# The experts' up products in one pass over both parts of the rows, with h_low on GpSimd

## The chip, the cores and the metric

One core of one Trainium2 chip. The metric is the device time of one execution in microseconds (us). The kernel before took 968.19 us (median of 3 runs, 966.38 to 971.39). The engines are called PE (TensorE matmul), DVE (VectorE), ACT (ScalarE), POOL (GpSimd) and SP (SyncE, which here issues the weight loads).

## What is computed

A gated cross attention, and then a gated mixture of experts over all 16 x 100 tokens of 512 features. The change touches only the experts:

```python
xs = x * gate                                # gate: sigmoid of the top router logit, top_k = 1
def body(acc, (wg, wd, e)):                  # 8 experts
    g, u = split(xs @ wg)                    # 512 -> 2 x 1024
    o = (silu(g) * u) @ wd                   # 1024 -> 512
    return acc + where(ids == e, o, 0)
routed = scan(body, 0, (w_gate_up, w_down))
shared = (silu(x @ sg) * (x @ su)) @ sd
x = x + tanh(g_ffn) * (routed + shared)
```

All inputs and outputs are fp32. The kernel multiplies in fp32r: it splits each operand into a high part (rounded by a copy to fp32r) and a low part (the difference), and adds the products high x high, high x low and low x high in PSUM.

## The kernel before, in words

The stage that matters is the last one, the routed experts (some 692 to 959 us of the profiled span). Each of the 8 experts is given the tokens routed to it, 2 tiles of 112 rows, 224 columns (SLOTS) once turned. The hidden size 1024 is worked off in four quarters of 256 (FQ), so there are 32 steps n = 4e + q. A step has two halves j = 0, 1 of 128 hidden features.

**PE** (`pe_routed`). In step n, for each half j: the gate product and the up product into PSUM banks 2j and 2j + 1, and after both halves the down product of step n - 1. The gate product (`pe_expert_gate`, L1648) already takes the rows' high and low part side by side: per 128 of the 512 input features one matmul of the weight's high part with 448 columns (rows high and low, L1660) and one of the weight's low part with the 224 columns of the rows' high part (L1662). The left half of the bank then lacks the right half, which must be added. The up product (`pe_gate_up`, L1613) takes three matmuls of 224 columns per 128 features (L1642), 12 in all, all added in PSUM. The down product (L1729) has two tiles of 6 matmuls. Ahead of q = 3 PE turns the next expert's rows (L1948).

**ACT** (`act_routed`), in this order in a step: copy_gate 0 (L1670: the right half of the bank into `hidden[0]`), part_high a, silu 0 (L1683), copy_gate 1, h_high 0 (L1703), part_high b, silu 1, h_high 1, part_high c. part_high (L1590) rounds one 128 x 1024 part of the next step's weights: a is gate, b is up, c is down. At q = 3 two rows_high (L1960) come first.

**DVE** (`dve_routed`): sum_gate 0 (L1677: left half of the bank plus the copy), part_low a (L1597), mult 0 (L1714: up from PSUM times the silu), h_low 0 (L1719), sum_gate 1, part_low b, mult 1, h_low 1, part_low c. At q = 3 two rows_low (L1967) come first; at q = 0 two add_residual (L2099) of the expert before come last.

**POOL** (`pool_routed`): for each expert the gather of the next expert's rows (L1991), the scatter of the last one's output (L2008) and the gather of this one's residual (L2001), all indirect DMAs.

**SP** loads a weight part of 512 KB when the part four before it in order has been split (`sp_load_part`, L1534).

Every engine works its list off in order, and semaphores tie them. Those that matter here: a product waits for part_low of its weights (`w_low`, L1621, L1654) and for the reader of its bank in the step before; h_high waits for mult; part_low for part_high; the down product for both h_low (L1726); copy_gate of half j waits for h_low of the same half in the step before, since `hidden[j]` is overwritten (L1669).

```python
    for i in range(k.KD):
        PE.matmul(bank[:, 0:2 * SLOTS].rearrange("p (x n) -> p x n", x=2), high[:, i, :], xs[:, :, i, 0:SLOTS],
                  start=(i == 0), stop=False)
        made = PE.matmul(bank[:, 0:SLOTS], low[:, i, :], xs[:, 0, i, 0:SLOTS], start=False, stop=(i == k.KD - 1))
```

Of the kernel before, what the change touches and what calls it, by code (L numbers as in the profile page):

```python
# [22 lines left out]
F32 = mybir.dt.float32  # L23
# [6 lines left out]
ACT = mybir.ActivationFunctionType  # L30
AX = mybir.AxisListType
MULT, ADD, SUB = ALU.mult, ALU.add, ALU.subtract

P = 128
# [135 lines left out]
def lay_out(k, nc, stack):  # L170
# [75 lines left out]
    k.w_raw = [carve(P, [PART], F32) for _ in range(2)]  # L246
    k.rows += [carve(P, [D], F32) for _ in range(2)]
    k.hidden = [carve(P, [max(k.width)], F32) for _ in range(2)]
    k.up_first = carve(P, [k.width[0]], F32)
    k.w_raw += [carve(P, [PART], F32), late("w_raw3", [P, PART], F32)]  # L250
    k.w_split = [[[carve_r(P, [PART], F32R) for _ in range(2)] for _ in range(3)]]
    k.xn_both = [xnT0, xnT1]
# [90 lines left out]
def sweep_semaphores(sem, name, it0, u0):  # L343
    r = Sweep()
    r.name, r.it0, r.u0 = name, it0, u0
    r.w_in = [sem(f"{name}_w_in{i}") for i in range(4)]
    r.w_high, r.w_low = sem(f"{name}_w_high"), sem(f"{name}_w_low")
    r.gu, r.silu, r.mult = sem(f"{name}_gu"), sem(f"{name}_silu"), sem(f"{name}_mult")
    r.h_high, r.h_low, r.routed_down = (sem(f"{name}_{n}") for n in ("h_high", "h_low", "routed_down"))
    r.gate_copied, r.gate_summed = sem(f"{name}_gate_copied"), sem(f"{name}_gate_summed")  # L350
    r.ids_in = sem(f"{name}_ids_in")
    r.rows_in = [sem(f"{name}_rows_in{i}") for i in range(4)]
    r.xt_turned, r.xt_high, r.xt_low = (sem(f"{name}_{n}") for n in ("xt_turned", "xt_high", "xt_low"))
    r.residual_in = [sem(f"{name}_residual_in{i}") for i in range(NT)]
    r.y_added = sem(f"{name}_y_added")
    r.y_out = [sem(f"{name}_y_out{i}") for i in range(NT)]
    return r
# [1245 lines left out]
def product_bank(r, it, j, which):  # L1603


    if it >= r.it0:
        return 2 * j + which
    if it < 2:
        return (((3, 2), (0, 2)), ((3, 5), (6, 7)))[it][j][which]
    return which  # L1610
# [34 lines left out]
        made.then_inc(r.gu, 1)  # L1645


def pe_expert_gate(k, r, PE, w, n, j):  # L1648


    it, u, xs = r.it0 + n, r.u0 + n, k.xn_both[n // k.NQ % 2]
    bank = k.bank[product_bank(r, it, j, 0)]
    high, low = (t[:].rearrange("p (k f) -> p k f", k=k.KD)[:, :, P * j:P * j + P] for t in k.w_split[u % 3][0])
    w.wait_ge(r.w_low, 3 * u + 1)  # L1654
    if n:
        w.wait_ge(r.gate_summed, 2 * n + j - 1)
    else:
        w.wait_ge(r.silu, 2 * it)
    for i in range(k.KD):
        PE.matmul(bank[:, 0:2 * SLOTS].rearrange("p (x n) -> p x n", x=2), high[:, i, :], xs[:, :, i, 0:SLOTS],  # L1660
                  start=(i == 0), stop=False)
        made = PE.matmul(bank[:, 0:SLOTS], low[:, i, :], xs[:, 0, i, 0:SLOTS], start=False, stop=(i == k.KD - 1))  # L1662
    made.then_inc(r.gu, 1)


def act_copy_gate(k, r, A, w, n, j):
    it = r.it0 + n
    w.wait_ge(r.gu, 4 * it + 2 * j + 1)
    w.wait_ge(r.h_low, 2 * it + j - 1)  # L1669
    A.activation(k.hidden[j][:, 0:SLOTS], k.bank[product_bank(r, it, j, 0)][:, SLOTS:2 * SLOTS],  # L1670
                 ACT.Copy).then_inc(r.gate_copied, 1)


def dve_sum_gate(k, r, V, w, n, j):
    gate = k.hidden[j][:, 0:SLOTS]
    w.wait_ge(r.gate_copied, 2 * n + j + 1)
    V.tensor_tensor(gate, k.bank[product_bank(r, r.it0 + n, j, 0)][:, 0:SLOTS], gate, ADD).then_inc(r.gate_summed, 1)  # L1677


def act_silu_expert(k, r, A, w, n, j):  # L1680
    gate = k.hidden[j][:, 0:SLOTS]
    w.wait_ge(r.gate_summed, 2 * n + j + 1)
    A.activation(gate, gate, ACT.Silu).then_inc(r.silu, 1)  # L1683
# [12 lines left out]
def act_h_high(k, r, A, w, it, j, width):  # L1696
    w.wait_ge(r.mult, 2 * it + j + 1)

    if 2 <= it < r.it0 + 2:
        w.wait_ge(k.shared_down, shared_downs(k, it - 1))  # L1700
    elif it >= r.it0 + 2:
        w.wait_ge(r.routed_down, NT * (it - r.it0 - 1))
    A.activation(k.hT[it % 2][0][:, j, 0:width], k.hidden[j][:, 0:width], ACT.Copy).then_inc(r.h_high, 1)  # L1703
# [314 lines left out]
def pe_routed(k, r, PE, w):  # L2018
    for n in range(k.E * k.NQ):
        e, q = divmod(n, k.NQ)  # L2020
        if q == k.NQ - 1 and e + 1 < k.E:
            for i in range(NT):
                pe_turn_rows(k, r, PE, w, e + 1, i)
        w.wait_ge(r.xt_low, NT * e + NT)
        for j in range(KF):
            pe_expert_gate(k, r, PE, w, n, j)
            pe_gate_up(k, r, PE, w, r.it0 + n, r.u0 + n, j, 1, k.xnT[e % 2], SLOTS)
        if n:
            pe_routed_down(k, r, PE, w, n - 1)
        elif r is k.first:  # L2030
            pe_shared_down(k, r, PE, w, 15, shared_points(16))
    pe_routed_down(k, r, PE, w, k.E * k.NQ - 1)
# [13 lines left out]
def act_routed(k, r, A, w):  # L2046
    for n in range(k.E * k.NQ):
        e, q = divmod(n, k.NQ)
        a, b, c = later_parts(k, r, n)
        if q == k.NQ - 1 and e + 1 < k.E:  # L2050
            for i in range(NT):
                act_rows_high(k, r, A, w, e + 1, i)
        act_copy_gate(k, r, A, w, n, 0)
        if a is not None:
            act_part_high(k, r, A, w, a)
        act_silu_expert(k, r, A, w, n, 0)
        act_copy_gate(k, r, A, w, n, 1)
        act_h_high(k, r, A, w, r.it0 + n, 0, SLOTS)
        if b is not None:
            act_part_high(k, r, A, w, b)  # L2060
        act_silu_expert(k, r, A, w, n, 1)
        act_h_high(k, r, A, w, r.it0 + n, 1, SLOTS)
        if n == 0 and r is k.first:
            act_shared_out(k, A, w, 15, shared_points(16))
        if c is not None:
            act_part_high(k, r, A, w, c)


def dve_routed(k, r, V, w):
    for n in range(k.E * k.NQ):  # L2070
        e, q = divmod(n, k.NQ)
        a, b, c = later_parts(k, r, n)
        if q == k.NQ - 1 and e + 1 < k.E:
            for i in range(NT):
                dve_rows_low(k, r, V, w, e + 1, i)
        dve_sum_gate(k, r, V, w, n, 0)
        if a is not None:
            dve_part_low(k, r, V, w, a)
        dve_mult(k, r, V, w, r.it0 + n, 0, SLOTS)
        dve_h_low(k, r, V, w, r.it0 + n, 0, SLOTS)  # L2080
        dve_sum_gate(k, r, V, w, n, 1)
        if b is not None:
            dve_part_low(k, r, V, w, b)
        dve_mult(k, r, V, w, r.it0 + n, 1, SLOTS)
        dve_h_low(k, r, V, w, r.it0 + n, 1, SLOTS)
        if n == 0 and r is k.first:
            dve_shared_add(k, V, w, 15, shared_points(16))
        if c is not None:
            dve_part_low(k, r, V, w, c)
        if n and q == 0:  # L2090
            dve_add_residual(k, r, V, w, e - 1)
    dve_add_residual(k, r, V, w, k.E - 1)
# [8 lines left out]


def pool_routed(k, r, G, w):
    for e in range(k.E):
        if e + 1 < k.E:
            pool_gather(k, r, G, w, e + 1)
        if e:
            pool_scatter(k, r, G, w, e - 1)
        pool_gather_residual(k, r, G, w, e)
    pool_scatter(k, r, G, w, k.E - 1)  # L2110

    for i in range(NT):
        w.wait_ge(r.y_out[i], 16 * k.E)
# [77 lines left out]
def sweep_again(k, nc, index):  # L2191
    r = k.again
    w = Waits(k.SP)
    for part in range(n_parts(k, r)):
        sp_load_part(k, r, k.SP, w, part)
    for i in range(NT):
        w.wait_ge(r.y_out[i], 16 * k.E)
    w = Waits(k.G)
    pool_gather(k, r, k.G, w, 0)
    pool_routed(k, r, k.G, w)  # L2200
    w = Waits(k.A)
    act_load_ids(k, r, k.A, w, index)
    for part in range(3):
        act_part_high(k, r, k.A, w, part)
    for i in range(NT):
        act_rows_high(k, r, k.A, w, 0, i)
    act_routed(k, r, k.A, w)
    w = Waits(k.V)
    for part in range(3):
        dve_part_low(k, r, k.V, w, part)  # L2210
    for i in range(NT):
        dve_rows_low(k, r, k.V, w, 0, i)
    dve_routed(k, r, k.V, w)
    w = Waits(k.PE)
    for i in range(NT):
        pe_turn_rows(k, r, k.PE, w, 0, i)
    pe_routed(k, r, k.PE, w)
    nc.all_engine_barrier()
    k.G.dma_reset()
    for s in [r.w_high, r.w_low, r.gu, r.gate_copied, r.gate_summed, r.silu, r.mult, r.h_high, r.h_low, r.routed_down, r.ids_in, r.xt_turned,  # L2220
              r.xt_high, r.xt_low, r.y_added, *r.w_in, *r.rows_in, *r.residual_in, *r.y_out]:
        k.G.sem_clear(s)
    nc.all_engine_barrier()
# [32 lines left out]
```

## Time and profile before

| | |
|---|---|
| median of 3 runs | 968.19 us (966.38 to 971.39) |
| profiled execution, its own time | 966.98 us |
| its span, first to last instruction | 964.8 us |
| mean granted TensorE clock | 0.997 |
| PE busy | 939.6 us (97%) |
| DVE busy | 626.7 us (65%) |
| ACT busy | 548.7 us (57%) |
| POOL busy | 171.6 us (18%) |

One execution was profiled; its time is 1.2 us under the median of the runs. Around the span lie 2.2 us. In the rows, a line gives the start in us from the span's start, the duration, the engine, the line of the kernel, the operation, the tensors it writes and reads, and in brackets the idle time before it with what ended it. An engine starts the next instruction before the busy time of the one before is over (the tails overlap), so that the spacing of starts is a little less than the duration where nothing is waited for. The halves of a step and the buffers all go by the names `arena_f` and `arena_f32r` in the rows, since those buffers are cut from two large ones.

### The profile page before, as it was taken

The page shows a single profiled execution, that of the slowest core. Times are in us where ns is not written, and L with a number is a line of the kernel's source. Part 1 is how long each engine was busy: PE and PEld are TensorE (multiplying, and loading weights), DVE is VectorE, ACT ScalarE, POOL GpSimd, SP SyncE. Part 2 cuts the span into 40 slices and gives each one's busy share as a digit, 9 for nine tenths or more (in the row PEclk, how much of TensorE's full clock was granted, in tenths as well). Part 3 has the DMA queues.
Part 4 walks back from the last instruction along what each step waited for, and adds up shares of the span by engine and source line. Part 5 has one row for each costly group of instructions (what it writes and reads, how often), then busy time and mean ns, then how long its engine had stood idle before and what let it go on. Part 6 is the DMA issues. An engine that isn't in the chain of part 4 may idle for free. (4 is left out here: it accounts for less than half of the span.)

```text
span 964.8 us, 24703 instructions
## 1 busy us (share of the span) xinstructions
PE 939.6 (97%) x10477; PEld 780.2 (81%) x10477; DVE 626.7 (65%) x1451; ACT 548.7 (57%) x839; POOL 171.6 (18%) x206
## 2 busy tenths in 40 slices
PE   5999999999999999999989999999999999999997
PEld 4777777777777777777777999999988888988886
DVE  6887655856568655776576444433577777777774
ACT  4677676677676777676723121222356666666653
POOL 1002221121113112113243200001011122112101
PEclk9999999999999999999999999999999999999999
DMA  8464534656455655456473210012487787778761
GB/s 312 114 116 88 116 86 89 139 96 107 90 105 128 154 96 111 79 99 140 101 157 109 62 44 22 23 44 75 132 251 218 223 247 235 217 235 237 231 200 60
DMA packets 175404, 129.98 MB, mean 135 GB/s; under 512 B 114611, under 2 KB 152499, under 8 KB 175289
## 3 DMA queue, kind: packets, MB, share of 16 engines
q1 hardware_dynamic: 165864, 108.60, 45.7%
q0 software_dynamic: 6544, 16.46, 5.6%
q10 hardware_dynamic: 2880, 3.29, 1.0%
q8 instruction: 85, 1.39, 0.6%
q14 instruction: 31, 0.25, 0.1%
HBM read 88.79 MB, written 13.56 MB: 106 GB/s over the span
## 5 line engine op out<-in xcount | busy, mean ns | idle before, releaser
L587 PE MATMUL bank<-arena_f32r 128*128 128x512 f32 (+1 forms) x1308 | 330.2, 402 | 12.2 <-DVE arena_f32r L952 10.7
L587 PEld LDWEIGHTS bank<-arena_f32r 128*128 128x128 f32 (+1 forms) x1308 | 231.1, 183 | 74.4 <-DVE arena_f32r L904 10.6
L782 ACT ACTIVATE probs<-score_banks 128x1600 f32<-128x1600 f32 x96 | 144.9, 1509 | 44.5 <-PE score_banks L606 43.9
L1703 ACT ACTIVATE hT_hi<-arena_f 128x224 fp32r<-128x224 f32 (+2 forms) x96 | 42.2, 441 | 116.6 <-DVE arena_f L1714 116.6
L1642 PE MATMUL bank<-xnT,arena_f32r 128*128 128x224 f32 (+1 forms) x720 | 102.3, 293 | 0.0
L1642 PEld LDWEIGHTS bank<-xnT,arena_f32r 128*128 128x128 f32 x720 | 97.1, 190 | 1.6 <-issue 0.3
L1714 DVE TENSOR_TENSOR arena_f<-bank,arena_f 128x224 f32<-128x224 f32 (+2 forms) x93 | 41.2, 443 | 65.2 <-PE bank L1642 64.7
L621 PEld LDWEIGHTS bank<-probs,values 128*17 128x17 f32 (+1 forms) x3072 | 63.4, 97 | 23.5 <-issue 21.1
L621 PE MATMUL bank<-probs,values 128*17 128x100 f32 (+1 forms) x3072 | 78.8, 250 | 0.9 <-ACT probs L782 0.8
L1060 POOL TENSOR_TENSOR heads_out<-heads_out,inv_sum 100x256 f32<-100x256 f32 x30 | 30.3, 1010 | 206.8 <-DVE inv_sum L1023 206.8
L1597 DVE TENSOR_TENSOR arena_f32r<-arena_f,arena_f32r 128x1024 fp32r<-128x1024 f32 x43 | 52.7, 1225 | 18.0 <-ACT arena_f32r L1590 18.0
L952 DVE TENSOR_TENSOR arena_f32r<-arena_f,arena_f32r 128x512 fp32r<-128x512 f32 (+1 forms) x48 | 31.9, 665 | 42.8 <-ACT arena_f32r L723 42.8
L1729 PE MATMUL score_banks<-arena_f32r,hT_hi 128*128 128x512 f32 (+2 forms) x184 | 58.0, 396 | 0.0
L1660 PE MATMUL bank<-xnT,arena_f32r 128*128 128x448 f32 x168 | 55.8, 377 | 0.0
L1729 PE MATMUL score_banks<-wdown_lo,hT_hi 128*112 128x512 f32 (+2 forms) x140 | 55.1, 394 | 0.0
L1729 PE MATMUL score_banks<-wdown_hi,hT_hi 128*112 128x512 f32 (+2 forms) x140 | 55.1, 393 | 0.0
L971 DVE TENSOR_REDUCE sumsq<-arena_f 128x32 f32<-128x512 f32 (+2 forms) x61 | 41.6, 682 | 19.8 <-ACT arena_f L739 19.8
L606 PEld LDWEIGHTS score_banks<-qT,kT 32*128 32x128 f16 x3072 | 37.1, 93 | 19.5 <-issue 17.4
L606 PE MATMUL score_banks<-qT,kT 32*128 32x100 f16 x3072 | 51.3, 204 | 0.2 <-ACT probs L782 0.2
L1693 ACT ACTIVATE arena_f<-bank 128x384 f32<-128x384 f32 (+1 forms) x29 | 14.7, 506 | 64.7 <-PE bank L1642 64.3
L1590 ACT ACTIVATE arena_f32r<-arena_f 128x1024 fp32r<-128x1024 f32 x43 | 45.1, 1048 | 8.4 <-DVE x_all L1887 8.4
L1887 DVE SCALAR_TENSOR_TENSOR x_all<-score_banks,gates,x_all 128x512 f32<-128x512 f32 (+1 forms) x52 | 38.6, 747 | 14.1 <-PE score_banks L1729 13.9
(270 smaller groups left out, 1786.1 us busy)
## 6 DMA issues: line engine op xcount, KB each, us to landing
arena_f<-L_ffn_w_gate_up SPq DMA_DIRECT2D x48, 512.0 KB, 4.4
arena_f<-L_ffn_w_down SPq DMA_DIRECT2D x24, 512.0 KB, 3.8
arena_f<-ctx SPq DMA_DIRECT2D x15, 722.0 KB, 4.3
w_raw<-L_ffn_w_gate_up SPq DMA_DIRECT2D x16, 512.0 KB, 4.3
w_raw<-L_ffn_w_down SPq DMA_DIRECT2D x8, 512.0 KB, 5.3
x_all<-x SPq DMA_DIRECT2D x8, 400.0 KB
x_rows<-x_all SPq DMA_DIRECT2D x4, 800.0 KB
x_all<-x_rows POOLq DMA_DIRECT2D x4, 768.0 KB, 6.8
```

The source lines that it names most:

```text
L587: product = PE.matmul(bank[0:rows, :], src[:, j, 0:rows], weight, start=(m == 0), stop=(m == 11))
L606: product = PE.matmul(k.score_banks[:, j, k.N * r:k.N * r + k.N], k.kT[b % 2][rows, block, P * t:P * t + P], k.qT[rows, part, block, queries],
L621: product = PE.matmul(k.bank[1][HW * j:HW * j + HD + 1, k.N * r:k.N * r + k.N], k.values[b % 2][0:m, t, 16 * z + GH * r + j, :], k.probs[n ...
L782: A.activation(k.probs[n % 2][:], k.score_banks[:, :, 0:GH * k.N].rearrange("p j (r n) -> p j r n", r=GH), ACT.Exp, scale=float(HD) ** -0. ...
L971: V.tensor_reduce(k.sumsq[b % 2][0:rows, sums_at(t), :], k.square[0:rows, :].rearrange("p (h d) -> p h d", d=HD), AX.X, ADD).then_inc(k.su ...
L1590: A.activation(k.w_split[u % 3][which][0][:], k.w_raw[part % 4][:], ACT.Copy).then_inc(r.w_high, 1)
L1597: V.tensor_tensor(low[:], k.w_raw[part % 4][:], high[:].bitcast(F32), SUB).then_inc(r.w_low, 1)
L1642: made = PE.matmul(bank[:, 0:width], weight[a][:, i, :], xs[x][:, i, 0:width], start=(i == 0 and n == 0), stop=(i == k.KD - 1 and n == 2))
L1660: PE.matmul(bank[:, 0:2 * SLOTS].rearrange("p (x n) -> p x n", x=2), high[:, i, :], xs[:, :, i, 0:SLOTS], start=(i == 0), stop=False)
L1703: A.activation(k.hT[it % 2][0][:, j, 0:width], k.hidden[j][:, 0:width], ACT.Copy).then_inc(r.h_high, 1)
L1714: V.tensor_tensor(h, up[:, 0:width], h, MULT).then_inc(r.mult, 1)
L1729: made = PE.matmul(bank[0:rows, :], k.hT[it % 2][h][:, j, r0:r0 + rows], weight[a][:, j, :], start=(first and j == 0 and n == 0), stop=(la ...
```

## The change

The up product takes the gate's form. `pe_expert_gate` becomes `pe_expert_products` with an argument `which` (0 gate, 1 up) and serves both. ACT copies the right half of the up bank too (`act_copy_up`, behind each silu), DVE adds the halves (`dve_sum_up`, ahead of each mult), and mult reads the sum from SBUF. h_low leaves DVE and goes to POOL (`pool_h_low`); POOL's gathers and scatters are spread over the quarters around it. The next up product into a bank waits for sum_up where it waited for mult. There is a new buffer pair, `up_parts`, in the place of `up_first`.

```diff
-    k.up_first = carve(P, [k.width[0]], F32)
+    k.up_first = carve(P, [max(k.width[0], 2 * SLOTS)], F32)
+    k.up_parts = [k.up_first[:, SLOTS * j:SLOTS * j + SLOTS] for j in range(KF)]
...
-def pe_expert_gate(k, r, PE, w, n, j):
+def pe_expert_products(k, r, PE, w, n, j, which):
...
-    bank = k.bank[product_bank(r, it, j, 0)]
-    high, low = (t[:].rearrange("p (k f) -> p k f", k=k.KD)[:, :, P * j:P * j + P] for t in k.w_split[u % 3][0])
-    w.wait_ge(r.w_low, 3 * u + 1)
+    bank = k.bank[product_bank(r, it, j, which)]
+    high, low = (t[:].rearrange("p (k f) -> p k f", k=k.KD)[:, :, P * j:P * j + P] for t in k.w_split[u % 3][which])
+    w.wait_ge(r.w_low, 3 * u + which + 1)
     if n:
-        w.wait_ge(r.gate_summed, 2 * n + j - 1)
+        w.wait_ge((r.gate_summed, r.up_summed)[which], 2 * n + j - 1)
     else:
-        w.wait_ge(r.silu, 2 * it)
+        w.wait_ge((r.silu, r.mult)[which], 2 * it)
...
+def act_copy_up(k, r, A, w, n, j):
+    it = r.it0 + n
+    w.wait_ge(r.gu, 4 * it + 2 * j + 2)
+    w.wait_ge(r.mult, 2 * it + j - 1)
+    A.activation(k.up_parts[j], k.bank[product_bank(r, it, j, 1)][:, SLOTS:2 * SLOTS], ACT.Copy).then_inc(r.up_copied, 1)
...
+def dve_sum_up(k, r, V, w, n, j):
+    up = k.up_parts[j]
+    w.wait_ge(r.up_copied, 2 * n + j + 1)
+    V.tensor_tensor(up, k.bank[product_bank(r, r.it0 + n, j, 1)][:, 0:SLOTS], up, ADD).then_inc(r.up_summed, 1)
+
+def dve_mult_expert(k, r, V, w, n, j):
+    it, h = r.it0 + n, k.hidden[j][:, 0:SLOTS]
+    w.wait_ge(r.silu, 2 * it + j + 1)
+    w.wait_ge(r.up_summed, 2 * n + j + 1)
+    V.tensor_tensor(h, k.up_parts[j], h, MULT).then_inc(r.mult, 1)
+
+def pool_h_low(k, r, G, w, n, j):
+    it = r.it0 + n
+    high, low = (t[:, j, 0:SLOTS] for t in k.hT[it % 2])
+    w.wait_ge(r.h_high, 2 * it + j + 1)
+    G.tensor_tensor(low, k.hidden[j][:, 0:SLOTS], high.bitcast(F32), SUB).then_inc(r.h_low, 1)
...
         for j in range(KF):
-            pe_expert_gate(k, r, PE, w, n, j)
-            pe_gate_up(k, r, PE, w, r.it0 + n, r.u0 + n, j, 1, k.xnT[e % 2], SLOTS)
+            for which in range(2):
+                pe_expert_products(k, r, PE, w, n, j, which)
...
         act_silu_expert(k, r, A, w, n, 0)
+        act_copy_up(k, r, A, w, n, 0)
         act_copy_gate(k, r, A, w, n, 1)
...
         act_silu_expert(k, r, A, w, n, 1)
+        act_copy_up(k, r, A, w, n, 1)
         act_h_high(k, r, A, w, r.it0 + n, 1, SLOTS)
...
-        dve_mult(k, r, V, w, r.it0 + n, 0, SLOTS)
-        dve_h_low(k, r, V, w, r.it0 + n, 0, SLOTS)
+        dve_sum_up(k, r, V, w, n, 0)
+        dve_mult_expert(k, r, V, w, n, 0)
         dve_sum_gate(k, r, V, w, n, 1)
...
-        dve_mult(k, r, V, w, r.it0 + n, 1, SLOTS)
-        dve_h_low(k, r, V, w, r.it0 + n, 1, SLOTS)
+        dve_sum_up(k, r, V, w, n, 1)
+        dve_mult_expert(k, r, V, w, n, 1)
...
 def pool_routed(k, r, G, w):
-    for e in range(k.E):
-        if e + 1 < k.E:
+    for n in range(k.E * k.NQ):
+        e, q = divmod(n, k.NQ)
+        if q == 0 and e + 1 < k.E:
             pool_gather(k, r, G, w, e + 1)
-        if e:
+        if q == 3:
+            pool_gather_residual(k, r, G, w, e)
+        pool_h_low(k, r, G, w, n, 0)
+        if q == 1 and e:
             pool_scatter(k, r, G, w, e - 1)
-        pool_gather_residual(k, r, G, w, e)
+        pool_h_low(k, r, G, w, n, 1)
     pool_scatter(k, r, G, w, k.E - 1)
```

## Rows read from the trace of the kernel before

**Rows 1.** The windows, one expert's four steps: busy time of each engine, instructions behind it.
```profile
817.00:849.60 32.60, 32.60 (x218) 29.34 (x217) 24.79 (x41) 20.53 (x39) 7.29 (x6) 1.00 0.77 227
```

**Rows 2.** The timeline of PE, a half step and the down product.
```profile
836.21 0.38 PE L1660 MATMUL bank<-xnT,arena_f32r 128*128 128x448 f32 x1
...
837.47 1.50 PE L1642 MATMUL bank<-xnT,arena_f32r 128*128 128x224 f32 x12
838.82 0.39 PE L1729 MATMUL score_banks<-wdown_hi,hT_hi 128*112 128x512 f32 x1
...
841.59 0.37 PE L1660 MATMUL bank<-xnT,arena_f32r 128*128 128x448 f32 x1
```

**Rows 3.** The timeline of DVE from step 0's last weight part to step 1's.
```profile
706.02 1.22 DVE L1597 TENSOR_TENSOR wdown_lo<-arena_f,wdown_hi 128x1024 fp32r<-128x1024 f32 x1 [2.10 <-ACT wdown_hi L1590]
707.16 0.38 DVE L1677 TENSOR_TENSOR arena_f<-bank,arena_f 128x224 f32<-128x224 f32 x1
707.46 1.22 DVE L1597 TENSOR_TENSOR arena_f32r<-arena_f,arena_f32r 128x1024 fp32r<-128x1024 f32 x1
708.60 0.38 DVE L1714 TENSOR_TENSOR arena_f<-bank,arena_f 128x224 f32<-128x224 f32 x1
709.44 0.40 DVE L1719 TENSOR_TENSOR arena_f32r<-arena_f,hT_hi 128x224 fp32r<-128x224 f32 x1 [0.46 <-ACT hT_hi L1703]
...
710.39 1.23 DVE L1597 TENSOR_TENSOR arena_f32r<-w_raw,arena_f32r 128x1024 fp32r<-128x1024 f32 x1 [0.25 <-ACT arena_f32r L1590]
...
713.32 1.23 DVE L1597 TENSOR_TENSOR arena_f32r<-arena_f,arena_f32r 128x1024 fp32r<-128x1024 f32 x1 [0.56 <-ACT arena_f32r L1590]
```

**Rows 4.** The timeline of ACT in the same step.
```profile
709.01 0.39 ACT L1703 ACTIVATE hT_hi<-arena_f 128x224 fp32r<-128x224 f32 x1 [0.80 <-DVE arena_f L1714]
709.31 1.04 ACT L1590 ACTIVATE arena_f32r<-w_raw 128x1024 fp32r<-128x1024 f32 x1
```

**Rows 5.** The timeline of DVE in the attention stage, chained small operations.
```profile
163.36 0.26 DVE L897 TENSOR_TENSOR rms_tmp<-rms_tmp,sumsq 128x96 f32<-128x96 f32 x1
163.65 0.26 DVE L898 SCALAR_TENSOR_TENSOR rms<-rms_tmp,rms 128x96 f32<-128x96 f32 x1
163.83 0.54 DVE L963 TENSOR_SCALAR x_all<-x_all,lx_mv,lx_rstd 128x512 f32<-128x512 f32 x1
...
474.05 0.42 DVE L1034 TENSOR_TENSOR heads_out<-bank,inv_sum 100x256 f32<-100x256 f32 x1
474.59 0.48 DVE L1039 SCALAR_TENSOR_TENSOR x_all<-heads_out,gates,x_all 100x256 f32<-100x256 f32 x1
```

**Rows 6.** The timeline of DVE at two borders between experts.
```profile
721.76 1.15 DVE L1967 TENSOR_TENSOR xnT<-score_banks,xnT 128x448 fp32r<-128x448 f32 x2
722.83 0.38 DVE L1677 TENSOR_TENSOR arena_f<-bank,arena_f 128x224 f32<-128x224 f32 x1
...
835.43 1.40 DVE L2099 SCALAR_TENSOR_TENSOR x_all<-score_banks,gates,x_all 112x512 f32<-112x512 f32 x2
836.75 0.38 DVE L1677 TENSOR_TENSOR arena_f<-bank,arena_f 128x224 f32<-128x224 f32 x1
```

**Rows 7.** The lines L1063, L1060 and L2001 of GpSimd: duration ns min/median/max, first and last start.
```profile
L1063 POOL TENSOR_TENSOR x_all<-x_all,heads_out x30: 682/690/1019, 73.9 to 470.0; 100x256 f32<-100x256 f32 x30
...
L1060 POOL TENSOR_TENSOR heads_out<-heads_out,inv_sum x30: 617/846/1601, 73.2 to 469.4; 100x256 f32<-100x256 f32 x30
...
L2001 POOL DMA_INDIRECT x_all<-x_rows,list_ids x16: 984/1250/1864, 708.9 to 943.5; - x16
...
DMA to landing us min/median/max: 3.5/5.4/7.2
```

**Rows 8.** The timeline of PE at step 2's first up product and in step 31.
```profile
712.05 1.50 PE L1642 MATMUL bank<-xnT,arena_f32r 128*128 128x224 f32 x12
...
949.00 0.39 PE L1642 MATMUL bank<-xnT,wup_hi 128*128 128x224 f32 x2
...
955.74 0.40 PE L1729 MATMUL score_banks<-wdown_hi,hT_hi 128*112 128x512 f32 x1
```

More of the change, by code:

```diff
@@ L350, in sweep_semaphores @@
     r.gate_copied, r.gate_summed = sem(f"{name}_gate_copied"), sem(f"{name}_gate_summed")
+    r.up_copied, r.up_summed = sem(f"{name}_up_copied"), sem(f"{name}_up_summed")
     r.ids_in = sem(f"{name}_ids_in")
@@ L2219, in sweep_again @@
     k.G.dma_reset()
-    for s in [r.w_high, r.w_low, r.gu, r.gate_copied, r.gate_summed, r.silu, r.mult, r.h_high, r.h_low, r.routed_down, r.ids_in, r.xt_turned,
+    for s in [r.w_high, r.w_low, r.gu, r.gate_copied, r.gate_summed, r.up_copied, r.up_summed, r.silu, r.mult, r.h_high, r.h_low, r.routed_down, r.ids_in, r.xt_turned,
               r.xt_high, r.xt_low, r.y_added, *r.w_in, *r.rows_in, *r.residual_in, *r.y_out]:
```

## The prediction

> **What bounds the kernel now.** I read the windows first, then the timelines of PE, DVE and ACT. Over one expert (817.0 to 849.6 us) PE is busy all 32.60 us, DVE 24.79 and ACT 20.53, at full clock [rows 1]. A step n takes PE 1.26 us for a gate product, 1.35 for an up product, each twice, and 2.77 for the down product of n-1: 7.99 us [rows 2]. So PE sets the pace. The second thing to see is how fast DVE and ACT would go if PE didn't hold them. The trace shows that once: after step 0 DVE is late and catches up. From the low part of step 0's down weights (706.02) to that of step 1 (713.32) are 7.30 us, and no wait of DVE in it ends on PE [rows 3]. These 7.30 us are one **ring** through both in-order queues: part_low a, mult 0, (ACT) h_high 0 and part_high b, part_low b, mult 1, (ACT) h_high 1 and part_high c, part_low c, sum_gate 0 of the next step. From start to start: 1.14, 0.41, 0.30 and 1.08 to part_low b (710.39), the same again (2.93 in all) to part_low c of step 1, and before both, from part_low c of step 0, 1.14 to sum_gate 0 and 0.30 to part_low a [rows 3, 4]. The ring has 0.69 us to spare against PE, and no more. PE can't run ahead of it: up of step n+1 waits for part_low b of step n.
>
> **The change, part by part.**
>
> *PE.* An up product of 12 matmuls of 224 columns becomes the gate's form, 4 of 448 and 4 of 224: 1.35 becomes 1.26, 0.09 us less. 64 products make 5.8 us, 0.18 a step; a step would take 7.81 us [rows 2]. The columns stay the same in number, only four weight loads go. At worst the saving is nothing, at best a third of 1.35, but the gate's row is the very form.
>
> *DVE, removed.* Two h_low of 0.40 us a step. The row of h_low 0 stands behind an idle stretch of 0.46 us that ends on ACT, and DVE idles again behind it until part_high b is done [rows 3]. It fills a hole of the ring: removing it gives the ring nothing.
>
> *DVE, added.* sum_up 0 and sum_up 1, PSUM and SBUF in, 224 columns, so sum_gate's 0.38 us. Each stands between a part_low and its mult, with no idle time before either, so both lie **on the ring**. Their price there is the spacing to a successor that reads the result. The trace has no such pair at 224 columns. Below: an independent successor of sum_gate starts after 0.30 [rows 3]. Above: a dependent one came after 0.54 where the first took 0.42 [rows 5]. Nearest in kind are the chained root steps: 0.26 us long, a dependent one starts after 0.29, an independent one after 0.18 [rows 5]. So duration plus 0.03: 0.41 us. The Trainium skill ("VectorE: DVE Perf Modes", The DRAIN you can't avoid) says a semaphore between chained operations costs nothing extra; by it sum_up would cost the independent 0.30. The root rows speak against it here.
>
> The ring becomes 7.30 + 2 x 0.41 = **8.12 us**, 0.31 over PE's 7.81, and over the 7.99 of before too. It passes PE.
>
> *DVE at an expert's borders.* rows_low (q = 3) takes 1.07 us on DVE and add_residual (q = 0) 1.32, both between part_low c and the next sum_gate [rows 6]: on the ring too. Until now an expert cost the ring 4 x 7.30 + 2.39 = 31.6 us, under PE's 32.6. Now it is 4 x 8.12 + 2.39 = 34.9, against PE's 31.9.
>
> *ACT.* Two copies more a step, some 0.36 us each (the gate's form is the same). copy_up 0 goes behind silu 0, while part_low a (1.14) runs; copy_up 1 behind silu 1, while part_low b runs. Both are done some 0.4 to 0.6 us before sum_up wants them: free in the steady state, 0.4 each in the last step, where no weight part covers them. The waits on the up product pass at once, since PE is ahead by then. mult now reads SBUF twice, as h_low did at 0.40 against mult's 0.38: nothing.
>
> *GpSimd.* 64 h_low. 100 x 256 from two SBUF inputs took 0.69 median [rows 7]; by columns 0.60 for 224, taken 0.61. Bounds: 0.3, and the 1.60 worst of the other form [rows 7]. It starts behind h_high, while DVE waits for part_high; PE wants it for the down product a step later: hidden, but for the last one. Its queue: gather e+1 stays at q = 0, the scatter moves into q = 1 between the two h_low, gather_residual to q = 3, ahead of h_low 0. Two issues take 2.0 to 3.7 us [rows 7], h_low waits behind them, and PE still has over 3 us. The x2 stores on which the first residual gather waits were done at 708.9 [rows 7], before q = 3 of expert 0 (some 719). The last residual gather starts near 966 and lands 5.4 us later [rows 7], before it is wanted at 974. SP's weight loads are released by part_low and move with the ring.
>
> **The sum.** Step 0 ends as before (x2's DMA issue and the shared adds set it), so part_low c of step 0 starts at 706.02. part_low b of step 1 then starts 0.41 later than its 710.39, at 710.80, and ends at 712.03. PE wants it at 712.05 less four up savings, 711.69 [rows 8]: the ring binds **from step 2 on**. To part_low b of step 30 there are 29 rings, 7 rows_low and 7 add_residual: 29 x 8.12 + 7 x 2.39 = 252.2, so it starts at 963.0 and ends at 964.2; up 0 of step 31 starts there, where it stood at 949.00 [rows 8]: 15.2 late. The last step: part_low c 966.35, sum_gate 0 967.5, silu 0 967.9, copy_up 0 968.2, sum_up 0 968.6, mult 0 969.0, sum_gate 1 969.3, silu 1 969.7, copy_up 1 970.0, sum_up 1 970.4, mult 1 970.8, h_high 1 971.2, h_low 1 971.7 to 972.3. The last down product stood at 955.74 [rows 8] and starts at 972.35: 16.6 late. What follows it is unchanged. The profiled execution took 966.98, so **983.6 us**; it lies 1.2 below the median of the three runs (968.19), whose sum would be 984.8.
>
> Own range of this case: with 0.30 for a sum_up, 29 x 2 x 0.11 = 6.4 less, 977; with 0.54, 7.5 more, 991.
>
> **Rivals.**
> *A. PE stays the bound* (faster). It needs a ring of at most 7.81, so each sum_up at most 0.25 us on it and nothing at the borders: 966.98 - 5.8 = 961.2. For it: PE is never idle now. Against: the 0.30 at which even an independent operation starts.
> *B. The rings' loss and PE's gain cancel* (within 0.5%, about what a measurement of this kernel can tell from no change): the borders are absorbed, because weights are split ahead, and a sum_up costs 0.30: 29 x (7.90 - 7.99) = -2.6, with the last step's +1.5 and up to 5 of the borders' 16.7 left over, some 966 to 971. Against: part_low b of step 1 had only 0.43 us before PE wanted it [rows 3, 8], so there is no store to absorb 2.39 us an expert.
> *C. GpSimd and DVE get in each other's way* (slower still). GpSimd's 100 x 256 multiply took from 0.62 to 1.60 us in this trace [rows 7]. Had h_low 1.60 and stopped DVE for as long as it overlaps the next part_low (0.65 us), each ring would grow by 1.3: 29 x 1.3 = 38, up to 1021. It decides once h_low passes 0.95 us, the gap between its start and part_low. The Trainium skill ("GPSIMD Engine Reference", Specifications) names contention with DVE instructions with two SBUF inputs, which part_low is. Against: at 0.61 us h_low is over before part_low starts.
>
> **Chances.** The forecast case 0.82; A 0.06; B 0.06; C 0.06. The range 974 to 992 is the forecast's own with a few us below, for a border term partly covered; A, B and C lie outside. Faster 0.06, same 0.06, slower 0.88.
>
> **What the profile after would show.** PE with some 20 us of idle time between 710 and 965, ended by DVE part_low of the up weights (L1597), none before 710; DVE's part_low c to part_low c at 8.12 us in a plain step, mult 0.41 behind sum_up; borders of 9.2 and 9.4; POOL h_low near 0.6 us, over before part_low b; PE's up products at 1.27. Wrong if plain steps are at 7.8 and PE has no idle time (A), if the spacing of sum_up and mult is under 0.3, or if part_low is longer than its 1.22 us (C).

## The result and the profile after

The changed kernel takes **989.81 us** (median of 4 runs, 989.44 to 991.11) against 967.9 for the kernel before: ratio 1.0212, 95% interval 1.0186 to 1.0239. It is slower by 22 us, where 16.6 were forecast; the time lies in the range given. Whether it is slower by more than 2% the interval leaves open. The profiled execution took 989.44 us over a span of 987.1.

Busy time of the engines over the whole span. PE's share fell from 97 to 95%. Its busy time didn't fall by what the up products save; why, the rows below show.

```profile
PE 940.3 (95%) x10221; PEld 770.6 (78%) x10221; DVE 625.2 (63%) x1451; ACT 560.3 (57%) x903; POOL 208.5 (21%) x270
```

The routed stage alone, from its first gate product to the end of the span: first the changed kernel, in the second fence the kernel before. The columns are the length, then the busy time of PE, PEld, DVE, ACT and POOL, the granted clock, the DMA share and GB/s.

```profile
692.20:987.10 294.90, 267.53 (x1489) 229.24 (x1487) 197.68 (x321) 173.46 (x364) 86.41 (x108) 1.00 0.64 197
```

```profile
692.00:964.80 272.80, 266.67 (x1745) 238.67 (x1743) 199.13 (x321) 162.03 (x300) 49.58 (x44) 1.00 0.71 213
```

The stage grew from 272.8 to 294.9 us, by 22.1: the whole difference. PE was idle in it for 6.1 us (272.80 - 266.67), behind its last product, and is now for 27.4. The granted clock is full in both.

The timeline of DVE in step 1, against [rows 3]:

```profile
706.35 1.23 DVE L1599 TENSOR_TENSOR wdown_lo<-arena_f,wdown_hi 128x1024 fp32r<-128x1024 f32 x1 [2.10 <-ACT wdown_hi L1592]
707.49 0.39 DVE L1686 TENSOR_TENSOR arena_f<-bank,arena_f 128x224 f32<-128x224 f32 x1
707.79 1.22 DVE L1599 TENSOR_TENSOR arena_f32r<-arena_f,arena_f32r 128x1024 fp32r<-128x1024 f32 x1
708.92 0.39 DVE L1692 TENSOR_TENSOR arena_f<-bank,arena_f 128x224 f32<-128x224 f32 x1
709.41 0.39 DVE L1699 TENSOR_TENSOR arena_f<-arena_f 128x224 f32<-128x224 f32 x1
709.72 0.38 DVE L1686 TENSOR_TENSOR arena_f<-bank,arena_f 128x224 f32<-128x224 f32 x1
711.22 1.23 DVE L1599 TENSOR_TENSOR arena_f32r<-w_raw,arena_f32r 128x1024 fp32r<-128x1024 f32 x1 [1.11 <-ACT arena_f32r L1592]
712.36 0.38 DVE L1692 TENSOR_TENSOR arena_f<-bank,arena_f 128x224 f32<-128x224 f32 x1
712.85 0.39 DVE L1699 TENSOR_TENSOR arena_f<-arena_f 128x224 f32<-128x224 f32 x1
714.64 1.23 DVE L1599 TENSOR_TENSOR arena_f32r<-arena_f,arena_f32r 128x1024 fp32r<-128x1024 f32 x1 [1.41 <-ACT arena_f32r L1592]
```

L1692 is sum_up, L1699 is mult. From part_low c to part_low c are 8.29 us where it was 7.30. mult starts 0.49 behind sum_up (708.92 to 709.41, 712.36 to 712.85), and that twice is the growth. Where h_low stood, DVE now idles for 1.11 and 1.41 us, and both stretches end on ACT's part_high.

The timeline of PE over one expert, those of its rows that have idle time before them:

```profile
819.57 0.47 PE L1662 MATMUL bank<-xnT,arena_f32r 128*128 128x448 f32 x1 [1.87 <-DVE arena_f32r L1599]
...
837.22 0.47 PE L1662 MATMUL bank<-xnT,wup_hi 128*128 128x448 f32 x1 [0.94 <-DVE wup_lo L1599]
...
845.51 0.48 PE L1662 MATMUL bank<-xnT,arena_f32r 128*128 128x448 f32 x1 [0.17 <-DVE arena_f32r L1599]
...
855.12 0.47 PE L1662 MATMUL bank<-xnT,arena_f32r 128*128 128x448 f32 x1 [1.57 <-DVE arena_f32r L1599]
```

Each stands at the first up product of a step, and each waits for part_low (L1599) of its weights. Three of the four steps have such a wait; in the one in which PE turns the next expert's rows (L1977), that takes up its spare time. From 819.57 to 855.12 are 35.55 us an expert, where 32.60 stood [rows 1]; 4 x 8.29 + 2.39 is 35.55. A plain step costs PE 8.29 (837.22 to 845.51). The first matmul behind such a wait takes 0.47 where others of its form take 0.38, and the tail of the last one ahead of it counts as busy alone (0.27 for a spacing of 0.10, since nothing overlaps it). Some 0.25 us a wait, and 23 waits, make some 6 us by this estimate, as much as the up products save. The experiment with ACT's order below, which has the same 1489 matmuls and no such wait, bears it out.

PE's first wait for part_low behind step 0, at up 0 of step 2:

```profile
712.50 0.47 PE L1662 MATMUL bank<-xnT,arena_f32r 128*128 128x448 f32 x1 [0.37 <-DVE arena_f32r L1599]
```

The timeline of PE in step 1, up 0, gate 1 and up 1 by their first matmul:

```profile
704.07 0.38 PE L1662 MATMUL bank<-xnT,wup_hi 128*128 128x448 f32 x1
...
705.35 0.38 PE L1662 MATMUL bank<-xnT,wgate_hi 128*128 128x448 f32 x1
...
706.63 0.38 PE L1662 MATMUL bank<-xnT,wup_hi 128*128 128x448 f32 x1
```

Both forms take 1.28 us here, 0.02 over [rows 2]; the up product has become as short as the gate's.

### The profile page after: what moved, and what is told of

Its sections match the earlier page's. It is cut to its first block and busy times, and to the rows that moved or that the text cites. A ratio compares the mean times of both kernels' runs of the same rounds, so it can differ in the third digit from the quotient of the medians.

```text
span 987.1 us, 24319 instructions
## 1 busy us (share of the span) xinstructions
PE 940.3 (95%) x10221; PEld 770.6 (78%) x10221; DVE 625.2 (63%) x1451; ACT 560.3 (57%) x903; POOL 208.5 (21%) x270
## 5 line engine op out<-in xcount | busy, mean ns | idle before, releaser
L1662 PE MATMUL bank<-xnT,arena_f32r 128*128 128x448 f32 x336 | 109.7, 380 | 13.4 <-DVE arena_f32r L1599 13.4
L1664 PE MATMUL bank<-xnT,arena_f32r 128*128 128x224 f32 x336 | 88.8, 264 | 0.0
L1662 PEld LDWEIGHTS bank<-xnT,arena_f32r 128*128 128x128 f32 x336 | 63.0, 187 | 23.2 <-DVE arena_f32r L1599 17.5
L1599 DVE TENSOR_TENSOR arena_f32r<-arena_f,arena_f32r 128x1024 fp32r<-128x1024 f32 x43 | 52.6, 1223 | 35.5 <-ACT arena_f32r L1592 35.5
L1664 PEld LDWEIGHTS bank<-xnT,arena_f32r 128*128 128x128 f32 x336 | 64.0, 191 | 0.7
L1743 DVE TENSOR_TENSOR arena_f<-bank,arena_f 128x384 f32<-128x384 f32 (+1 forms) x29 | 16.7, 576 | 64.1 <-PE bank L1644 64.1
L608 PEld LDWEIGHTS score_banks<-qT,kT 32*128 32x128 f16 x3072 | 37.1, 93 | 19.5 <-issue 17.4
```

Source lines behind the costliest of these rows:

```text
L608: product = PE.matmul(k.score_banks[:, j, k.N * r:k.N * r + k.N], k.kT[b % 2][rows, block, P * t:P * t + P], k.qT[rows, part, block, queries],
L1599: V.tensor_tensor(low[:], k.w_raw[part % 4][:], high[:].bitcast(F32), SUB).then_inc(r.w_low, 1)
```

## The experiments

The profiled executions reach the routed stage at 691.8 to 697.5 us, though what runs ahead of it is the same in all these kernels. So besides the times, the length of the routed stage in each profile is given, first gate product to the end of the span: 272.8 for the kernel before, 294.9 for the changed one.

**The order of ACT (e3_act_order, e4_before_act_order).** part_high b is put ahead of h_high 0, part_high c ahead of h_high 1, in the changed kernel and in the kernel before:

```diff
-        act_h_high(k, r, A, w, r.it0 + n, 0, SLOTS)
         if b is not None:
             act_part_high(k, r, A, w, b)
+        act_h_high(k, r, A, w, r.it0 + n, 0, SLOTS)
...
+        if c is not None and n:
+            act_part_high(k, r, A, w, c)
         act_h_high(k, r, A, w, r.it0 + n, 1, SLOTS)
...
-        if c is not None:
+        if c is not None and not n:
             act_part_high(k, r, A, w, c)
```

> The changed kernel with ACT's order altered alone: part_high b ahead of h_high 0 and part_high c ahead of h_high 1. Theory (the ring through both queues bounds the changed kernel): the ring is cut, because part_high no longer waits for mult through h_high; what is left on DVE a step is three part_low of 1.14, two sum_up of 0.49, two mult and two sum_gate of 0.30, 4.6 to 5.6 us, under PE's 7.8. PE binds again and its saving shows: 967.9 - 5.8 = 962 (960 to 964), and no wait of PE on part_low. Rival GpSimd (its h_low or its queue costs the time): the order of ACT changes nothing there, 985 to 990. Rival work (DVE and ACT have too much to do, wherever it stands): nothing is removed, 985 to 990.

> The kernel before with the same change of ACT's order, to tell what the order gives by itself. Theory: PE bounds it before and after, 967.9 within 1.5. Rival (the order helps everything, and the new up form has no part in it): 962.

Measured: 964.02 us with the new form (ratio to the kernel before 0.9952, 0.9934 to 0.9971), 967.9 without it (0.9994, 0.9974 to 1.0014). The routed stage took 266.9 us (697.5 to 964.4), 28.0 less than in the changed kernel and 5.9 less than in the kernel before; in the other kernel 272.7. Not one instruction was removed. First the stage in this kernel; then one of the three rows of its gate and up products (L1662), and below it the list of what the matmuls of this line waited for, which is empty:

```profile
697.50:964.40 266.90, 261.32 (x1489) 229.29 (x1487) 200.16 (x321) 174.79 (x364) 121.40 (x108) 0.99 0.72 218
```

```profile
L1662 PE MATMUL bank<-xnT,wup_hi x88: 372/377/380, 709.3 to 952.7; 128*128 128x448 f32 x88
its engine sat idle before it (us, times) until:
who waited for it (us, times):
```

No PE wait on part_low is left. So the ring was the bound. Without it the new form saves about what PE's rows had promised (5.8 us): 5.9 by the stage, 5.35 by PE's busy time in it (266.67 to 261.32), and 4.2 by the medians (968.21, the kernel before beside these runs, to 964.02), whose interval reaches from 3 to 6. The median lies at the upper end of the 960 to 964 expected. And with the waits gone PE's busy time is 6.2 us less than in the changed kernel (267.53). The 0.5% is a gain over the kernel before that neither edit gives alone.

**h_low moved by itself (e1_hlow_dve, e2_before_hlow_pool).** The changed kernel with h_low back on DVE, and the kernel before with h_low on GpSimd:

```diff
         dve_mult_expert(k, r, V, w, n, 0)
+        dve_h_low(k, r, V, w, r.it0 + n, 0, SLOTS)
...
-        pool_h_low(k, r, G, w, n, 0)
```

```diff
         dve_mult(k, r, V, w, r.it0 + n, 0, SLOTS)
-        dve_h_low(k, r, V, w, r.it0 + n, 0, SLOTS)
...
+        pool_h_low(k, r, G, w, n, 0)
```

and the same for half 1.

> The changed kernel with h_low back on DVE, each behind its mult as before, GpSimd's queue without it. Theory: h_low 0 fits into DVE's idle time ahead of part_low b (1.11 us), h_low 1 into that ahead of part_low c (1.41 us): ring unchanged at 8.3, 990 within 2; the last step ends some 0.3 earlier. Rival GpSimd: the time was lost there, so 968 to 975. Rival work: 64 more DVE instructions of 0.3 to 0.4 us, 20 us more, 1008.

> The kernel before with h_low on GpSimd and GpSimd's queue as in the change, up products as before. Theory: PE has 0.7 us to spare a step and h_low has a step to be done in: 968 within 1. Rival GpSimd: slower by 5 to 20 us.

Measured: 993.75 us (ratio 1.0256, 1.0223 to 1.0289; stage 296.5) and 968.56 (0.9996, 0.9977 to 1.0015; stage 272.7). The first was expected within 2 of 990 and came out above that; its profiled run took 990.91. DVE in its step 1:

```profile
707.04 1.23 DVE L1599 TENSOR_TENSOR wdown_lo<-arena_f,wdown_hi 128x1024 fp32r<-128x1024 f32 x1 [2.10 <-ACT wdown_hi L1592]
...
710.11 0.39 DVE L1699 TENSOR_TENSOR arena_f<-arena_f 128x224 f32<-128x224 f32 x1
710.96 0.39 DVE L1748 TENSOR_TENSOR arena_f32r<-arena_f,hT_hi 128x224 fp32r<-128x224 f32 x1 [0.46 <-ACT hT_hi L1732]
711.27 0.38 DVE L1686 TENSOR_TENSOR arena_f<-bank,arena_f 128x224 f32<-128x224 f32 x1
711.91 1.23 DVE L1599 TENSOR_TENSOR arena_f32r<-w_raw,arena_f32r 128x1024 fp32r<-128x1024 f32 x1 [0.26 <-ACT arena_f32r L1592]
...
715.34 1.23 DVE L1599 TENSOR_TENSOR arena_f32r<-arena_f,arena_f32r 128x1024 fp32r<-128x1024 f32 x1 [0.56 <-issue]
```

The ring is 8.30 (707.04 to 715.34) with 64 more instructions on DVE: h_low (L1748) fills the idle stretch. The 1.6 us more of the stage lie ahead of the ring and behind it: part_low c of step 0 starts 14.9 us into the stage and not 14.2, because h_low 1 delays the shared adds, and in the last step h_low 0 stands in front of sum_gate 1. My expectation that the last step would end earlier was wrong. GpSimd's part is worth nothing by itself, for or against.

**One half (e5_one_half).** Half 0 keeps the old up form, half 1 has the new one:

```diff
-            for which in range(2):
-                pe_expert_products(k, r, PE, w, n, j, which)
+            pe_expert_products(k, r, PE, w, n, j, 0)
+            if j:
+                pe_expert_products(k, r, PE, w, n, j, 1)
+            else:
+                pe_gate_up(k, r, PE, w, r.it0 + n, r.u0 + n, j, 1, k.xnT[e % 2], SLOTS)
...
-        act_copy_up(k, r, A, w, n, 0)
...
-        dve_sum_up(k, r, V, w, n, 0)
-        dve_mult_expert(k, r, V, w, n, 0)
+        dve_mult(k, r, V, w, r.it0 + n, 0, SLOTS)
```

> The changed kernel with the new up form in half 1 alone; half 0 has 12 matmuls of 224 columns and mult from PSUM, as before. Theory: one sum_up on the ring in the place of two: 7.30 + 0.50 = 7.80, and 7.80 x 4 + 2.39 = 33.6 an expert against PE's 32.2; part_low b of step 30 comes 29 x 0.5 = 14.5 us earlier than in the changed kernel, so 975 to 976. Rival (a fixed cost of the new path, such as GpSimd's): 985 or more.

Measured: 974.22 us (ratio 1.0066, 1.0044 to 1.0089), stage 278.9.

```profile
711.21 1.22 DVE L1599 TENSOR_TENSOR wdown_lo<-arena_f,wdown_hi 128x1024 fp32r<-128x1024 f32 x1 [2.10 <-ACT wdown_hi L1592]
...
719.01 1.23 DVE L1599 TENSOR_TENSOR arena_f32r<-arena_f,arena_f32r 128x1024 fp32r<-128x1024 f32 x1 [1.41 <-ACT arena_f32r L1592]
```

The ring is 7.80, to the hundredth. The time is some 1 us under what was expected: the estimate counted the 29 rings, and the sum_up that is gone is gone from the first and the last step too. Each sum_up is worth 0.5 us of ring.

**The same instruction on the ring and in the hole (e6_extra_on_ring, e7_extra_in_hole).** One more DVE instruction of 224 columns (an added scratch product, outside the kernel's own computation), 64 times:

```diff
+def dve_extra(k, r, V, w):
+    same = k.ident32[:, 0:TR].unsqueeze(1).to_broadcast([P, NT, TR])
+    V.tensor_tensor(k.scratch[:].rearrange("p (a b) -> p a b", a=NT), same, same, MULT)
...
+        dve_extra(k, r, V, w)
         dve_sum_up(k, r, V, w, n, 0)
```

and in the other kernel

```diff
         dve_sum_gate(k, r, V, w, n, 1)
+        dve_extra(k, r, V, w)
```

> The changed kernel with one more independent DVE instruction of 224 columns (ident32 times itself into a scratch buffer) ahead of each sum_up, so on the ring. Theory: each costs the spacing of 0.30: ring 8.9, 29 x 0.6 = 17.4, with the last step's up to 0.6: 1007 to 1008. Rival (DVE isn't on the path): 990.

> The same extra instruction, the same number of times, behind sum_gate 1 and behind mult 1, where DVE idles until part_low. Theory: nothing, 990 within 1.5. Rival work (DVE's total counts): as with the extra instruction on the ring, 1007.

Measured: 1010.58 us (ratio 1.0437, 1.0381 to 1.0493; stage 313.5, 18.6 more than the changed kernel) and 991.51 (1.024, 1.0191 to 1.0289; stage 294.8, nothing more). The first came out over the 1007 to 1008 expected (its two executions took 1008.27 and 1012.89). From part_low b of step 1 to that of step 30 it took 17.4 us more than the changed kernel, as forecast; the expectation left out three extras ahead of that, 0.9 us. In the hole, DVE:

```profile
711.52 0.38 DVE L1687 TENSOR_TENSOR arena_f<-bank,arena_f 128x224 f32<-128x224 f32 x1
711.82 0.38 DVE L1698 TENSOR_TENSOR scratch<-ident 128x224 f32<-128x224 f32 x1
713.01 1.23 DVE L1600 TENSOR_TENSOR arena_f32r<-w_raw,arena_f32r 128x1024 fp32r<-128x1024 f32 x1 [0.81 <-ACT arena_f32r L1593]
```

The same work costs 0.3 us each or nothing, by its place alone: the idle time ahead of part_low shrank from 1.11 to 0.81, and part_low comes when it came.

**GpSimd longer than the hole (e8_hlow_twice).** Each h_low on GpSimd is preceded by the same subtraction into a scratch buffer:

```diff
     w.wait_ge(r.h_high, 2 * it + j + 1)
+    w.wait_ge(r.pool_extra, 2 * n + j)
+    G.tensor_tensor(k.scratch[:], k.hidden[j][:, 0:SLOTS], high.bitcast(F32), SUB).then_inc(r.pool_extra, 1)
     G.tensor_tensor(low, k.hidden[j][:, 0:SLOTS], high.bitcast(F32), SUB).then_inc(r.h_low, 1)
```

> The changed kernel with each h_low on GpSimd preceded by the same subtraction into a scratch buffer, so that GpSimd works some 1.35 us behind each h_high and overlaps part_low by 0.4 us. Theory: part_low keeps its 1.22 us, ring 8.3, and only the last step grows by 0.7: 990 to 991. Rival C of the prediction (GpSimd and DVE get in each other's way): part_low or GpSimd's subtraction longer where they overlap; up to 0.4 us for each of 58 part_low, 1010.

Measured: 1012.85 us (ratio 1.046, 1.0404 to 1.0517), stage 313.3, 18.4 more than the changed kernel. My theory expected nothing here and fell. DVE and POOL in step 1 of this kernel (L1600 is part_low, L1709 h_low):

```profile
716.32 1.48 DVE L1600 TENSOR_TENSOR arena_f32r<-w_raw,arena_f32r 128x1024 fp32r<-128x1024 f32 x1 [1.11 <-ACT arena_f32r L1593]
717.72 0.38 DVE L1693 TENSOR_TENSOR arena_f<-bank,arena_f 128x224 f32<-128x224 f32 x1
```

```profile
716.04 0.67 POOL L1709 TENSOR_TENSOR arena_f32r<-arena_f,hT_hi 128x224 fp32r<-128x224 f32 x1
```

part_low takes 1.48 us where it took 1.22; when it starts, GpSimd is 0.39 us from its end. Two of these a step and 29 steps make 15 us; the last step adds 0.7. The other 2.7 of the 18.4 lie in seven steps, those in which GpSimd issues a scatter between its two h_low. It is late by that, part_low c meets the first of its two subtractions (L1708) just begun, and the second one holds up the next part_low a too. One of the seven, two rows of DVE and, in the second fence, one of POOL:

```profile
757.49 1.74 DVE L1600 TENSOR_TENSOR wdown_lo<-arena_f,wdown_hi 128x1024 fp32r<-128x1024 f32 x1 [1.41 <-ACT wdown_hi L1593]
...
759.46 1.39 DVE L1600 TENSOR_TENSOR wgate_lo<-arena_f,wgate_hi 128x1024 fp32r<-128x1024 f32 x1
```

```profile
757.44 0.70 POOL L1708 TENSOR_TENSOR scratch<-arena_f,hT_hi 128x224 f32<-128x224 f32 x1
```

In most of the seven part_low c takes 1.69 and not 1.48, part_low a 1.38 and not 1.21: 0.38 us a step. This is the mechanism of rival C, at its forecast place: it doesn't act in the changed kernel only because h_low (0.67) is over before part_low starts.

The clock isn't what lengthens the rings. It is lower in this kernel, 0.97 in the stage, and 0.96 in the kernel with the extra instruction on the ring. One stretch stands here for the rest: TensorE was granted 1.2 GHz (0.50) from some 984 to 987.6, after it had been idle for 2.00 us before the matmul at 983.20; it worked without a pause until the clock was full again.

```profile
985.00:986.00 1.00, 1.00 (x5) 0.94 (x4) 0.66 (x1) 1.00 (x3) 0.98 (x3) 0.50 0.47 139
```

From part_low b to part_low b are 9.17 us there (981.68 to 990.85), and 9.16 at the same place of an earlier expert (867.93 to 877.09), where the clock stayed at 1.00.

In the kernel with ACT's new order, GpSimd and DVE overlap the other way round, part_low first:

```profile
857.99 1.23 DVE L1599 TENSOR_TENSOR arena_f32r<-arena_f,arena_f32r 128x1024 fp32r<-128x1024 f32 x1 [0.24 <-ACT arena_f32r L1592]
```

```profile
858.32 1.42 POOL L1706 TENSOR_TENSOR arena_f32r<-arena_f,hT_hi 128x224 fp32r<-128x224 f32 x1 [2.77 <-ACT hT_hi L1732]
```

There part_low keeps 1.23 and h_low takes 1.42 in the place of 0.67. Whoever comes second pays. There the second one is GpSimd, which has time.

**What the spacing of sum_up and mult is made of (e10_silu_wait_first, e11_sum_from_sbuf).** In one kernel the wait of mult for silu is put in front of sum_up, so that one wait is left in front of mult. In the other sum_up adds the copy to itself, which leaves out the high rows' part of up:

```diff
+    w.wait_ge(r.silu, 2 * (r.it0 + n) + j + 1)
     w.wait_ge(r.up_copied, 2 * n + j + 1)
     V.tensor_tensor(up, k.bank[product_bank(r, r.it0 + n, j, 1)][:, 0:SLOTS], up, ADD).then_inc(r.up_summed, 1)
```

```diff
-    V.tensor_tensor(up, k.bank[product_bank(r, r.it0 + n, j, 1)][:, 0:SLOTS], up, ADD).then_inc(r.up_summed, 1)
+    V.tensor_tensor(up, k.up_parts[j], up, ADD).then_inc(r.up_summed, 1)
```

> The changed kernel with mult's wait for silu put ahead of sum_up, where it holds anyway, so that mult is preceded by one wait, the one for sum_up. Theory W (the 0.08 us over the forecast in the spacing of sum_up and mult come from the second wait in front of mult): spacing 0.41, ring 8.14, 29 x 0.16 = 4.6 less, 985. Theory P (they come from sum_up itself, which reads PSUM): spacing 0.49, 990 within 1.5.

> The changed kernel with sum_up adding the copy to itself in SBUF in the place of the bank's left half (the high rows' products are left out of up), order and waits unchanged. Theory P: spacing 0.41, ring 8.14, 985. Theory W: spacing 0.49, 990.

Measured: 985.13 us (ratio 1.0167, 1.0134 to 1.02; stage 290.5, 4.4 less than the changed kernel) and 990.42 (1.0221, 1.018 to 1.0263; stage 296.6, of which the 1.7 over the changed kernel lie behind the last product, at the output's last stores). DVE in both, sum_up and mult, in the first with the part_low ahead of them:

```profile
707.52 1.22 DVE L1599 TENSOR_TENSOR arena_f32r<-arena_f,arena_f32r 128x1024 fp32r<-128x1024 f32 x1
708.66 0.38 DVE L1693 TENSOR_TENSOR arena_f<-bank,arena_f 128x224 f32<-128x224 f32 x1
709.07 0.39 DVE L1700 TENSOR_TENSOR arena_f<-arena_f 128x224 f32<-128x224 f32 x1
```

```profile
708.45 0.38 DVE L1692 TENSOR_TENSOR arena_f<-arena_f 128x224 f32<-128x224 f32 x1
708.94 0.39 DVE L1699 TENSOR_TENSOR arena_f<-arena_f 128x224 f32<-128x224 f32 x1
```

0.41 us with one wait in front of mult, 0.49 with two, whether sum_up reads PSUM or not. Theory W holds. In front of sum_up the second wait costs next to nothing: sum_up starts 1.14 behind part_low, where it started 1.13 behind it in the changed kernel.

**The new form without GpSimd (e9_act_order_hlow_dve).** ACT's new order and h_low on DVE, both as above.

> The changed kernel with ACT's new order and with h_low back on DVE, so the new up form without GpSimd. Theory: with the ring cut DVE has room for two h_low of 0.3 to 0.4 us a step (some 6.3 of 7.8 us in use), PE binds, 962 to 965, within 0.2% of the kernel with ACT's order alone. Rival (GpSimd is needed, since h_low 0 again stands between mult 0 and sum_gate 1 and waits for ACT, which now does part_high b first): the ring closes again through h_low: mult 0, h_high 0, h_low 0, sum_gate 1, silu 1, part_high c, part_low c; then over 970, with PE waiting for part_low.

Measured: 963.55 us (ratio 0.995, 0.9933 to 0.9967), stage 268.3. PE waited for part_low once:

```profile
PEld bank L1662 <- DVE arena_f32r L1599: 0.8, 1, 0.8
...
PE bank L1662 <- DVE arena_f32r L1599: 0.5, 1, 0.5
```

The part of the change that went to GpSimd isn't needed. The two best versions, this one and the changed kernel with ACT's order alone (964.02), can't be told apart. Both beat both kernels.

## Why the prediction was right

**The bound.** Right: DVE and ACT together set the pace from step 2 on. PE's first wait (712.50) stands where it was forecast, with 0.37 us of idle time, and cutting the ring brought the whole loss back.

**PE's saving.** Right: 0.09 us a product, 5.8 in all, forecast; with the ring cut, 5.9 by the stage of one profile, 4.2 by the medians.

**The price of a sum_up.** Right in mechanism, the size was off: "So duration plus 0.03: 0.41 us" measured 0.49. This is the term that made 983.6 out of 989.4 (the profiled execution's own time): 29 x 2 x 0.08 = 4.6 of the 5.8 us missed. The root steps from which I took the 0.03 have a single wait in front; mult has two. The pair that had 0.54 behind 0.42, which I kept as the upper end [rows 5], would have given duration plus 0.12, so 0.50. With the second wait taken away, 0.41 was measured; that this is also why the root steps gave 0.03 is not tested. The rest of the miss, from the rows: 0.4 us ahead of part_low b of step 1 (711.22 and not 710.80), 0.8 in the 29 rings, of which 0.35 come from a single mult that started late, 0.4 in the last step, and 0.5 the other way behind the last down product.

```profile
816.49 0.39 DVE L1699 TENSOR_TENSOR arena_f<-arena_f 128x224 f32<-128x224 f32 x1 [0.46 <-DVE arena_f L1692]
```

**The hole.** Right: h_low's removal from DVE gave nothing, and putting it back cost the ring nothing.

**The borders.** Right: 2.39 us an expert, on the ring; 35.55 us an expert agree with it to the hundredth.

**GpSimd.** h_low takes 0.67 and not 0.61, off the path but for the last step. Two rows of this line in the changed kernel (duration min/median/max, first and last start):

```profile
L1706 POOL TENSOR_TENSOR hT_lo<-arena_f,hT_hi x32: 660/671/678, 698.7 to 971.3; 128x224 fp32r<-128x224 f32 x32
L1706 POOL TENSOR_TENSOR arena_f32r<-arena_f,hT_hi x32: 656/669/677, 710.3 to 977.8; 128x224 fp32r<-128x224 f32 x32
```

**The last step.** Forecast at 1.4 us (16.6 late behind 15.2); PE waited 1.63 there:

```profile
978.56 0.46 PE L1758 MATMUL score_banks<-wdown_hi,hT_hi 128*112 128x512 f32 x1 [1.63 <-POOL arena_f32r L1706]
```

**The rivals.** A fell: a plain step takes 8.29 us and not 7.81, and no spacing behind a sum_up was under 0.41. B fell: nothing of the borders was absorbed. C isn't what happened, but its mechanism is real, as the doubled h_low shows. The gap I gave, 0.95 us, is the point at which the two begin to overlap (0.91 to 0.92 in the rows); no run tried lengths around it. Its price is 0.26 us there, for an overlap of 0.39.

## What to carry to other kernels

When one engine is busy all the time, look for a stretch of the trace in which the others catch up, and read from it how fast their queues turn by themselves: here that was 7.30 against 7.99 us, and the change asked for 0.98 more. What matters is where in the queues an instruction stands: the same 64 instructions cost 18.6 us on the ring and nothing in its hole. And where a ring runs through two in-order queues, look for an instruction that stands behind a wait it doesn't need (here part_high behind h_high): moving it was worth 26 us, after which the change gave its 0.5%.

## What the runs showed of the hardware that I had not expected

Three spacings of two DVE instructions of 224 columns, each 0.38 us long: 0.30 when the second is independent, 0.41 when it waits for the first, 0.49 when it has another wait in front as well, though that one had been met about 1 us before. Behind a part_low, 1.22 us long, the second wait doesn't show (1.13 and 1.14). The Trainium skill ("VectorE: DVE Perf Modes", The DRAIN you can't avoid) has it that a semaphore between chained operations costs nothing extra, as measured there on eight copies; here the waiting successor came 0.11 to 0.19 later than an independent one.

GpSimd and DVE, each with two inputs in SBUF, hold each other up, and the one that comes second pays: part_low grew from 1.22 to 1.48 us behind a subtraction of GpSimd with 0.39 us to go, that subtraction from 0.67 to 1.42 behind a part_low with 0.90 to go. The Trainium skill ("GPSIMD Engine Reference", Specifications) names this contention; the traces agree.
